# Attention weights normalised by ScalarE head by head instead of by VectorE in one product

## What is computed

```python
scores = jnp.einsum('bhsr,bhlr->bhsl', q_r, k_r)      # 16 heads, 128 x 128 each
attn = jax.nn.softmax(scores, axis=-1)
ctx_c = jnp.einsum('bhsl,bld->bhsd', attn, kv_r)
ctx_lat = jnp.einsum('bhsd,hkd->bhsk', ctx_c, w_kc_kv)
```

## Time and profile before

| | us |
|---|---|
| median of 3 runs | 562.46 |
| lowest and highest | 562.05, 563.54 |
| the profiled execution | 561.04 |
| its span in the trace | 559.2 |

### The profile page before, as it was taken

How to read it: one execution, slowest core, us unless ns; L and a number is a source line. 1 busy time by engine, 2 the same in 40 slices (tenths; PEclk the granted TensorE clock), 3 DMA queues, 4 the chain that set the end, 5 groups by cost and what they waited for, 6 DMA issues and landing times.

```text
span 559.2 us, 10332 instructions
## 1 busy us (share of the span) xinstructions
PE 451.7 (81%) x3272; PEld 372.0 (67%) x3280; DVE 408.5 (73%) x733; ACT 319.8 (57%) x700; POOL 238.5 (43%) x165
## 2 busy tenths in 40 slices
PE   5999966448657747667899999999999999997833
PEld 2437766345546637546788988898988988896612
DVE  0947998089999999999654576777777676676443
ACT  1539748788888888888234353434535353434310
POOL 2300563397797897986123223322232223322010
PEclk9999978757758668777999999999999999999665
DMA  8721684421011101111200000000000000000000
GB/s 296 301 75 40 182 256 163 175 60 39 29 45 40 28 28 39 36 38 28 80 11 2 10 2 2 19 0 19 0 19 0 9 9 0 19 0 19 1 10 10
DMA packets 19268, 29.89 MB, mean 53 GB/s; under 512 B 1712, under 2 KB 14384, under 8 KB 18288
## 3 DMA queue, kind: packets, MB, share of 16 engines
q1 hardware_dynamic: 19248, 29.64, 15.8%
HBM read 23.34 MB, written 6.29 MB: 53 GB/s over the span
## 4 chain that ended last, share of the span: by engine, by line
PE 39%; DVE 24%; issue 19%; ACT 7%; POOL 6%; DMA 3%; DVEq 2%; POOLq 0%; SPq 0%; ACTq 0%
PE ps L361 34%; DVE ps L1113 7%; DVE reg_b L1120 4%; POOL reg_b L958 2%; POOL reg_b L937 2%; DVE ps L1110 2%; PE ps L558 2%; POOL small L942 1%; ACT reg_b L816 1%; DVE reg_b L1173 1%; DMA reg_a<-w_kr 1%; DMA reg_a<-a_log 1%; DVE x1T L1059 1%; DVE reg_b L1172 1%; PE ps L464 1%
## 5 line engine op out<-in xcount | busy, mean ns | idle before, releaser
L937 POOL TENSOR_TENSOR reg_b<-reg_c,reg_a 128x1024 f32<-128x1024 f32 x56 | 130.3, 2370 | 18.1 <-ACT reg_a L724 17.6
L958 POOL TENSOR_TENSOR reg_b<-reg_b 128x768 f32<-128x768 f32 x32 | 58.0, 1812 | 140.1 <-DVE reg_b L1173 107.4
L464 PE MATMUL ps<-ident,hc 128*128 128x128 f32 x452 | 83.9, 340 | 24.2 <-ACT hc L740 23.8
L361 PE MATMUL ps<-x1T,Mw 128*128 (+1 forms) x768 | 93.5, 278 | 0.0
L740 ACT ACTIVATE hc<-reg_b,bc 128x512 f32<-128x512 f32 x112 | 80.2, 716 | 23.3 <-PE ps L464 11.5
L464 PEld LDWEIGHTS ps<-ident,hc 128*128 128x128 f32 x452 | 66.0, 176 | 39.2 <-ACT hc L740 39.2
L361 PEld LDWEIGHTS ps<-x1T,Mw 128*128 128x128 f32 x768 | 88.2, 192 | 3.4 <-DVE reg_b L1173 0.3
L1120 DVE SCALAR_TENSOR_TENSOR reg_b<-reg_c,bc,ps 128x512 f32<-128x512 f32 x112 | 82.8, 745 | 0.0
L816 ACT ACTIVATE reg_b<-ps,small 128x128 f32<-128x128 f32 x128 | 45.3, 366 | 40.0 <-DVE small L1178 39.3
L1113 DVE TENSOR_TENSOR ps<-ps,reg_b 128x512 f32<-128x512 f32 x96 | 66.5, 698 | 0.0
L731 ACT ACTIVATE ps<-reg_b 128x512 f32<-128x512 f32 x112 | 64.9, 581 | 0.0
(11 more groups left out here) (141 smaller groups left out, 743.2 us busy)
## 6 DMA issues: line engine op xcount, KB each, us to landing
reg_a<-a_log SPq DMA_DIRECT2D x4, 1024.0 KB, 5.6
reg_a<-w_q SPq DMA_DIRECT2D x1, 2048.0 KB, 11.7
zs_dram<-reg_c SPq DMA_DIRECT2D x4, 512.0 KB, 3.3
ud_dram<-Nw SPq DMA_DIRECT2D x4, 512.0 KB, 4.9
reg_a<-w_o SPq DMA_DIRECT2D x1, 2048.0 KB, 11.0
ud_t<-ud_dram SPq DMA_DIRECT2D x8, 256.0 KB, 2.7
zs_t<-zs_dram SPq DMA_DIRECT2D x8, 256.0 KB, 2.6
reg_a<-w_kcq SPq DMA_DIRECT2D x1, 1536.0 KB, 14.9
```

Of the source, the lines that this page charges most:

```text
L361: return pe.matmul(o, l, r, start=start, stop=stop)
L464: return pe.matmul(o, src, ident[:, :], start=start, stop=stop, is_transpose=True, skip_group_check=True)
L937: pool.tensor_tensor(dA[:, g % RING], delta_r[:, bass.ds(t, 1), :].to_broadcast([P, SA, DI]), Abc[:, g * SA:(g + 1) * SA, :], ALU.mult).th ...
L958: pool.tensor_tensor(rq[:, g % 2].rearrange("p a c n -> p (a c n)"), pc[:, g % 2].rearrange("p a c n -> p (a c n)"), psn[:, g % 2].rearran ...
```

## The change

VectorE's product is dropped; it only computes the reciprocals. ScalarE multiplies the four heads in place, one ACTIVATE with a per-row scale each, ahead of `take_prob` in the same slot. VectorE's reciprocal also waits until the normalisation of the group before is done, since `rsum` has one buffer.

```diff
@@ ScalarE
+            def normalize(k, g):
+
+                act.wait_ge(rcp, k + 1)
+                for h in range(HG):
+                    last = act.activation(prob[:, g % 2, h, :], prob[:, g % 2, h, :], ACT.Copy, scale=rsum[:, h:h + 1])
+                last.then_inc(nrm, 1)
+
             def take_prob(k, g):
                 act.wait_ge(ptm, k + 1)
                 need(act, cxm, k - 1)
...
                     if merge and g == 3:
                         ffn(t - 1, 5)
                     if (lag or g >= 2) and (proj or g < 2):
+                        normalize(k - 2, (g - 2) % G)
                         take_prob(k - 2, (g - 2) % G)
@@ VectorE
             def normalize(k, g):
 
                 dve.wait_ge(pexp, k + 1)
+                need(dve, nrm, k)
                 dve.reciprocal(rsum, sums[:, g % 2]).then_inc(rcp, 1)
-                dve.wait_ge(rcp, k + 1)
-                dve.tensor_tensor(prob[:, g % 2], prob[:, g % 2], rsum.unsqueeze(2).to_broadcast([P, HG, P]),
-                                  ALU.mult).then_inc(nrm, 1)
```

## The result

| | before | after |
|---|---|---|
| median, us | 562.25 (4 runs) | 581.01 (4 runs, 580.21 to 583.16) |
| span of the profiled execution | 559.2 | 579.6 |
| ratio, with its 95% interval | | 1.0335 [1.0302, 1.0367] |

A forecast was written before the change was run, and what follows sets the result against it. The prediction took TensorE to bound the attention slots, 31.64 us a tile. Its terms summed to 21.0 us, taking the profiled 561.04 us to 582.0, stated as 583 for the median, range 575 to 591.

The forecast's parts named there:

- plain slots, four: Slots without an FFN copy, two each in tiles 0 and 1: TensorE starts turn_prob 0.42 us later, 1.7 us.
- slot 1, six: Slot 1 of tiles 2 to 7: multiplications queue behind the FFN copy, turn_prob 1.31 us later each, 7.9 us.
- slots 3 and 0, five pairs: Slot 3 and the next tile's slot 0: 0.87 plus 0.42 us late, 1.29 a pair, 6.45 us.
- slot 2, seven: Slot 2: normalisation ready 2.2 us before TensorE needs it, covered by merge_heads, so 0.
- first pair: Slot 3 of tile 1 and slot 0 of tile 2: TensorE had next to no wait to use up, 1.9 us.
- last pair: The pair ending in the drain, where TensorE waits for VectorE: only VectorE's side counts, 1.1 us.
- drain, slot 1: Slot 1 of the drain: multiplications follow TensorE's transposes at the lower clock and a copy, delaying turn_prob 2.0 us.
- The queue: ScalarE in slots 0, 1, 3: multiplications stand behind an FFN copy awaiting TensorE's transposes; matters more than their price.
- The clock: Rival in the slots: TensorE's waits lower the granted clock for part of the stretch, another 23 us, 606; chance 0.05.
- Faster: Rival: normalisation is ready by the end of to_latent everywhere, 4.2 us less, 558; chance 0.02.
- All products exposed: Rival: each of 32 normalisations costs its bare 0.61 us, slot 2 too, +19.5 us, 582; chance 0.05.
- The pairs free: Rival in slots 3 and 0: VectorE's saved 0.61 us pays twice, so pairs cost nothing, 12.7 us, 575; chance 0.09.

The follow-up runs named there:

- e2: The kernel before with VectorE's product left out and nothing in its place, only the reciprocals computed; 556.32 us, ratio 0.9903.
- e5: The kernel before with slot 3's row maxima moved ahead of the last two quantisation steps on VectorE; 554.85 us, ratio 0.9877.
- e9: The kernel before with the change in slot 3 alone, VectorE multiplying in the other slots; 562.25 us, ratio 1.0001.
- e3: The changed kernel with two more 128x128 copies, results unused, ahead of ScalarE's four multiplications; 594.93 us, ratio to before 1.0596.
- e4: The changed kernel with two buffers for the reciprocals, so VectorE waits only for the normalisation one group earlier; 582.93 us, ratio to before 1.0343.
- e12: The changed kernel with slot 3's row maxima moved ahead of the last two quantisation steps; 578.56 us, ratio to before 1.0285.
- e13: The changed kernel with ScalarE's multiplications ahead of the FFN copies and slot 3's row maxima ahead of the last two quantisation steps; 564.84 us, ratio to before 1.0048.
- e7: The kernel before with the change in slot 1 alone, VectorE multiplying in the other slots; 574.12 us, ratio 1.0221.
- e6: The kernel before with the change in slot 2 alone, VectorE multiplying in the other slots; 563.23 us, ratio 1.0029.
- e1: The changed kernel with ScalarE's four multiplications moved ahead of the FFN copy in slots 0, 1 and 3; 566.24 us, ratio to before 1.008.
- e11: The kernel before with GpSimd's rope sum in slot 3 held back until that slot's quantisation is done; 556.47 us, ratio 0.9892.

## Why the prediction was right, point by point

Forecast 583, measured 581.01, within the stated 575 to 591; the sum 21.0 us, against 20.4 us by the spans. By its terms, from the lateness at each turn_prob in the profiled execution:

| term | forecast | measured |
|---|---|---|
| stage before the slots | 0 | 0.33 |
| plain slots, four | 1.7 | 1.28 |
| slot 1, six | 7.9 | 7.36 |
| slots 3 and 0, five pairs | 6.45 | 5.72 |
| slot 2, seven | 0 | -0.36 |
| first pair | 1.9 | 1.79 |
| last pair | 1.1 | 0.45 |
| drain, slot 1 | 2.0 | 1.73 |
| drain, behind the last turn_prob | 0 | 2.07 |
| sum | 21.0 | 20.4 |

That the sum came within 0.6 us is in part luck. The terms that were forecast measured 18.0 us together, 3.0 less than forecast, and two stretches that were put at nothing, the stage before the slots and the end of the drain, gave 2.4 back.

- What it removes and what bounds: right. Without any product 6 us are gained, nearly all in slot 0, slot 3 and the drain. Slot 3's 0.23 us a tile the prediction did not see, as its row marks no wait.
- The price: 396 ns forecast, 390 measured; four in 1.27 us, where I took 1.30. The page of the Trainium skill that the prediction named, ScalarE: Activation LUTs (What ACT_TABLE_LOAD costs), came to 1.27, and the trace agrees with that.
- The queue: right, and the largest part. The hand-over to TensorE took 0.05 us in slots 1 and 3 (405.39 + 1.27 = 406.66, loads 406.71), where I took 0.08 to 0.10. This and the price make up the 0.08 us by which slots 1 and 3 were forecast too dear.
- Slot 3: L1211 (now L1217) did have to wait for TensorE, as the step says. That VectorE stays 0.42 us late was wrong. Against slot 2's turn_prob L1217 began 0.34 us later than before, but the rounding step behind it fell from 0.77 to 0.30 us, as GpSimd's sum had ended (the row at 427.47), and the row maxima then began 0.13 us earlier than before (428.01 against 418.99). This does not matter in the loop, where slot 0 hangs on the FFN copy. It does in the drain: the last pair cost 0.45 instead of 1.1. This is the mis-sized term.
- Slot 2 is covered: right, by 16 products of merge_heads (the prediction says eight). Its -0.05 us comes from the measure: it stands only in the kernels whose slot 1 waits, where the loads start behind the wait and not during the products ahead of them; the +0.05 us of slot 1 in e2, e5 and e9 is its counterpart.
- Slot 1 of the drain: the queue was right, the clock was not. TensorE's transposes took 0.66 us (540.12, before the clock fell), where I had taken the 1.11 us of the kernel before; with those I estimate the term at 2.2 us (1.73 + 0.45), not 1.73.
- The clock: right in the slots, wrong in the drain. The rival wanted a fall of the clock within the slots, and there was none, though TensorE was busy for only 92% of them, as it had foreseen (first row of the windows below, up to the last turn_prob of the loop). But the merge_heads of the drain began at the lower level. Groups of TensorE's loads in the drain, before and then after:

```profile
L361 PEld LDWEIGHTS ps<-Pw,reg_b 128*128 128x128 f32 x16 | 3.0, 190 | 1.2 <-ACT reg_b L829 0.9
```

```profile
L361 PEld LDWEIGHTS ps<-Pw,reg_b 128*128 128x128 f32 x16 | 4.6, 296 | 1.9 <-ACT reg_b L836 0.9
```

and the windows of TensorE after (columns as in the earlier trace rows), the second over the first of these products:

```profile
270.00:526.84 256.84, 237.37 (x2153) 1.00 0.03 8
545.92:549.34 3.42, 2.94 (x12) 0.50 0.00 0
```

  The 16 loads took 296 ns each in the mean instead of 190. The group lasted 5.6 us in place of 3.3, behind the same wait of 0.88 us, and these 2.3 us fill the last term of the table. The granted clock was 0.50 for the first 4.7 us of it, the lower of the two levels; in the kernel before it was 1.00 over the whole group (528.72 to 532.04 us), having risen at about 528.6. The stretch from the last turn_prob to the end was 36.7 to 37.1 us in the change, in e3, e4 and e12, 36.0 us in e13 (its 16 loads took 280 ns each), and 33.7 to 34.9 us in the kernel before and in the other eight. Why these five kernels meet the lower level there stays open. In the drain's slot 1 e7's products wait 2.25 us before the FFN transposes and 1.85 before turn_prob, exactly as the change's, and its merge_heads ran at 1.00, so these waits alone are not the cause. In e7 the clock fell at about 531.1 us, at the start of the FFN transposes, and was up again at 537.9, just before merge_heads at 538.12. In the change it fell behind them, at about 541.4, and merge_heads began at 546.98.
- The rivals. Faster, and a change that does nothing: no. All products exposed forecasts 19.5 us, close to the total by chance; slot 2 and e3 exclude it. The pairs free: no, a pair costs 1.14 us. But e9 shows that its idea holds for slot 3 alone.
- The added wait on nrm, "nothing": nothing in the change, but it seems to be worth 0.08 us a tile where VectorE is the late engine (e6 and e7).

## What to carry to other kernels

The price of a moved operation is set by the queue that it joins: look at what stands ahead of it there and what that waits for, before comparing durations. Here moving the same four instructions cost 19 us behind a copy and 4 us ahead of it. A wait that an engine already has swallows a loss of its size (slot 3 alone cost nothing), but only once, and only if nothing new is late in the same slot. And where a profile shows one short idle time of the bounding engine in each turn of a loop, as the 0.60 us here, ask which instruction in the late engine's queue could stand elsewhere: moving one by two places gave 1.2%, nearly half of it in the drain.

## What the runs showed of the hardware that was not expected

A VectorE operation SBUF to SBUF, 128x256 float32 with immediates (L1220), took 0.77 us when it began during GpSimd's 1.81 us sum (L958), and 0.28 to 0.30 us where it began as the sum ended or later, as in the loops of the change and of e1, e3, e4, e5, e9, e11, e12 and e13. In the kernel before it ends 0.15 us after GpSimd does: 385.14 + 1.81 = 386.95, and 386.33 + 0.77 = 387.10. That holds whenever it begins: 1.19 us into the sum it took 0.77 us, 1.33 us into it 0.64 (e2), 1.55 us into it 0.41 (the first one of e1), and each time it ended 0.14 to 0.16 us behind the sum. So it is held until GpSimd is done, not slowed in proportion; the sum itself took 1.81 us with or without it. Its neighbour ahead (L1218), which reads PSUM, took 0.48 us in either case.

That is the rule of the Trainium skill (SBUF — State Buffer, SBUF: two separate sides): VectorE in its two-port modes, or with two SBUF inputs where GpSimd reads SBUF too, and GpSimd share a port pair, and whoever comes second is blocked until the other is done. The trace agrees in that the later one is held to the end of the earlier. No row names the mode in which L1220 runs. In slot 0 it was worth 0.49 of the kernel's 0.60 us of wait (e11), and nothing on the page's busy shares points to it. Only a mean that is too long for its shape does, 773 ns at 256 columns where the same line takes 427 at 512 (groups of the kernel before by shape, from 330 to 505 us, which is five tiles):

```profile
L1220 DVE TENSOR_SCALAR reg_b<-reg_b 128x256 f32<-128x256 f32 x5 | 3.9, 773 | 0.2
L1220 DVE TENSOR_SCALAR reg_b<-reg_b 128x512 f32<-128x512 f32 x6 | 2.6, 427 | 0.2
```
